# Half of the context's features transposed in 32x32 blocks by VectorE from a second copy, in place of TensorE's transposes

## The reference, cut to what matters

```
x: (16, 64, 512)   ctx: (16, 512, 512)                 # 16 batches, 64 queries, 512 context rows, 512 features
q = layernorm(x) @ Wq.T + bq
k = ctx @ Wk.T + bk ;  v = ctx @ Wv.T + bv
scores = (q @ k.T) / sqrt(512)
keep the 32 largest scores of each query, the rest -inf; attn = softmax(scores)
x = x + (attn @ v) @ Wo.T + bo
```

## Time and profile before

| | |
|---|---|
| median of 3 runs | 445.98 us (445.91 to 446.12) |
| the profiled execution's own time | 447.19 us |
| its span, first to last instruction | 445.4 us |
| granted TensorE clock | 1.00 (2.4 GHz) |
| PE busy | 433.1 us, 97% of the span |
| DVE busy | 257.6 us, 58% |
| ACT busy | 205.6 us, 46% |
| DMA | 49.97 MB, mean 112 GB/s |

### The profile page before, as it was taken

How to read it: one execution, slowest core, us unless ns; L and a number is a source line. 1 busy time by engine, 2 the same in 40 slices (tenths; PEclk the granted TensorE clock), 3 DMA queues, 4 the chain that set the end, 5 groups by cost and what they waited for, 6 DMA issues and landing times.

```text
span 445.4 us, 5681 instructions
## 1 busy us (share of the span) xinstructions
PE 433.1 (97%) x2045; PEld 312.7 (70%) x2045; DVE 257.6 (58%) x519; ACT 205.6 (46%) x305; POOL 111.1 (25%) x163
## 2 busy tenths in 40 slices
PE   5999999999999999899999999999999999999996
PEld 2587644557565655478888888887888888888884
DVE  2988535567766777769987335548753333533334
ACT  1796852645464466538875445435531111111110
POOL 2600440000000002010008603334256633333330
PEclk9999999999999999999999999999999999999999
DMA  6999920675414542225649000000000000200002
GB/s 192 409 379 391 371 80 0 208 266 190 179 46 155 190 156 105 94 96 188 213 166 177 13 22 4 0 0 1 0 1 0 0 1 1 95 1 1 1 0 94
DMA packets 26844, 49.97 MB, mean 112 GB/s; under 512 B 6208, under 2 KB 6208, under 8 KB 25792
## 3 DMA queue, kind: packets, MB, share of 16 engines
q1 hardware_dynamic: 26816, 49.61, 31.7%
HBM read 47.49 MB, written 2.11 MB: 111 GB/s over the span
## 4 chain that ended last, share of the span: by engine, by line
PE 78%; DMA 7%; DVE 6%; ACT 4%; issue 2%; SPq 1%; POOL 1%; DVEq 0%; ACTq 0%
PE bank L1189 10%; PE bank L1191 10%; PE bank L1190 10%; PE bank L1605 7%; PE bank L1603 7%; PE bank L1589 6%; PE bank L1590 6%; PE bank L1384 6%; PE bank L1370 5%; PE bank L1398 5%; PE bank L1297 3%; PE bank L1196 3%; DMA wab<-w1T 2%; DMA wab<-w2T 2%; DVE ln_s L779 1%
## 5 line engine op out<-in xcount | busy, mean ns | idle before, releaser
L754 ACT ACTIVATE g<-bank,b1c 128x512 f32<-128x512 f32 x32 | 22.0, 688 | 92.0 <-PE bank L1605 92.0
L1169 DVE CAST g_hi<-g 128x512 fp32r<-128x512 f32 x32 | 14.0, 436 | 74.7 <-ACT g L754 74.6
L417 POOL TENSOR_TENSOR ln_rs<-ln_ve,neg_half 128x1 f32<-128x1 f32 x24 | 14.9, 620 | 146.2 <-DVE ln_ve L783 145.8
L1603 PE MATMUL bank<-xt_lo,w1s 128*128 128x512 f32 x128 | 50.8, 397 | 0.0
L1605 PE MATMUL bank<-xt_hi,w1s 128*128 128x512 f32 x128 | 50.7, 396 | 0.0
L1589 PE MATMUL bank<-w2s,g_lo 128*128 128x512 f32 x128 | 50.3, 393 | 0.2 <-DVE g_lo L1171 0.2
L1590 PE MATMUL bank<-w2s,g_hi 128*128 128x512 f32 x128 | 50.0, 390 | 0.0
L569 ACT ACTIVATE mt<-bank 128x512 f32<-128x512 f32 x56 | 30.1, 600 | 28.6 <-PE bank L1370 28.6
L464 POOL TENSOR_SCALAR w2s<-w2t 128x512 fp32r<-128x512 int8 x32 | 19.9, 622 | 65.8 <-PE bank L1590 65.8
L1384 PE MATMUL bank<-mt,qT 128*64 128x512 f32 x128 | 31.1, 605 | 0.0
L1589 PEld LDWEIGHTS bank<-w2s,g_lo 128*128 128x128 f32 x128 | 24.0, 188 | 6.1 <-issue 0.6
(11 more groups left out here) (231 smaller groups left out, 1015.3 us busy)
## 6 DMA issues: line engine op xcount, KB each, us to landing
ctxr<-ctx SPq DMA_DIRECT2D x8, 1024.0 KB, 10.9
ctx<-ctx SPq DMA_DIRECT2D x8, 1024.0 KB, 7.7
wab<-w1T SPq DMA_DIRECT2D x4, 1024.0 KB, 11.5
wab<-w2T SPq DMA_DIRECT2D x4, 1024.0 KB, 9.0
wgraw<-wgT SPq DMA_DIRECT2D x4, 1024.0 KB, 6.5
wst<-w1T SPq DMA_DIRECT2D x4, 1024.0 KB, 4.7
wst<-w2T SPq DMA_DIRECT2D x4, 1024.0 KB, 5.2
resid<-x SPq DMA_DIRECT2D x4, 512.0 KB, 6.9
```

What stands on the lines that cost most here:

```text
L1603: pe.matmul(bank[n % 2][:, :], w1s[:, n % 2, d, :], xt_lo[:, d, half(n // FC)], start=(d == 0), stop=False)
```

## The change

The context's features 0 to 255 are loaded a second time, in another layout: `raw_load(i)` loads for pair `i`, in four DMAs of 32 partitions each, rows in blocks of 32, so that partition 32g+j holds row 32m+j of each block m with the features 64g to 64g+63. Such a DMA moves 256 bytes at a time. DVE then transposes 32x32 blocks (`block_part`, two instructions of 128x512 for a quarter of the features, four a pair), which gives the turned context for features 0 to 255 in another order of the features; `m1_hi`, `m1_lo` and `sum_k` are put into the same order (`blocks_first`, `in_blocks`), for which each `m1` part is split into two instructions of 256 columns on ACT and on DVE. PE turns only the features 256 to 511: four chunks a pair, two in each half of an iteration. ACT copies all four; DVE's `mt1_part` is gone. The steps of the score take the pieces in the order 2, 0, 3, 1: first and third from ACT, second and fourth from DVE.

The second copy takes two of the eight tiles, so that three pairs of the context are held and not four; `ctx_load` waits for a `weigh` one iteration later than before relative to its use, and `raw_load` for the transposes that free its tile. DVE's list in an iteration is reordered (in the diff). `wgraw`, `wst`, `qfT`, `conv`, the `toe` tiles and `woutraw` move to other tiles, with waits to match; `woutraw` now waits for the last `ternary`.

```diff
+BLK = 32
...
-        (ctxr,), (wgraw,), (wk_lo,), (qfT, conv), (wst,) = region(
+        (ctxr,), (wgraw,), (wk_lo, wgq_lo), (conv, qfT), (wst,) = region(
             [("ctxr", [P, 4, SC, D], F32)],
             [("wgraw", [P, 4, DC, D], F32)],
-            [("wk_lo", [P, DC, D], F32R)],
-            [("qfT", [P, DC, B * T], F32), ("conv", [P, NT, D], F32)],
+            [("wk_lo", [P, DC, D], F32R), ("wgq_lo", [P, DC, D], F32R)],
+            [("conv", [P, NT, D], F32), ("qfT", [P, DC, B * T], F32)],
             [("wst", [P, 4, FF], F32)])
         (ctx2,), \
             (xn6, targ, tdec, habs, cpr, wpar, wtmp, cpl, tpos), \
-            (wv_hi, wv_lo, wgq_lo), (toe_hi, toe_lo, _, woutraw), (wave_hi, wave_lo) = region(
+            (wgraw2, wv_hi, wv_lo), (wst2,), (_, woutraw, toe_hi, toe_lo), (wave_hi, wave_lo) = region(
             [("ctx2", [P, 4, SC, D], F32)],
             [("xn6", [P, NT - 2, D], F32), ("targ", [P, H, CT], F32), ("tdec", [P, H, CT], F32), ("habs", [P, H, NC], F32),
              ("cpr", [P, P], F32), ("wpar", [P, 3, H], F32), ("wtmp", [P, 6, H], F32), ("cpl", [P, H], F32),
              ("tpos", [P, CT], F32)],
-            [("wv_hi", [P, DC, D], F32R), ("wv_lo", [P, DC, D], F32R), ("wgq_lo", [P, DC, D], F32R)],
-            [("toe_hi", [P, H, P], F32R), ("toe_lo", [P, H, P], F32R), ("apart", [P, DC, D], F32),
-             ("woutraw", [P, DC, D], F32)],
+            [("wgraw2", [P, 2, DC, D], F32), ("wv_hi", [P, DC, D], F32R), ("wv_lo", [P, DC, D], F32R)],
+            [("wst2", [P, 2, FF], F32)],
...
+        def ctx_home(b):
+            return (2, 3, 5, 6, 0, 1)[b % 6]
...
+            n = ctx_home(b)
+            return (ctx2 if n < 4 else ctxr)[:, n % 4, :, :]
+        def raw_pair(i):
+            return ctxr[:, 3 * (i % 2), :, :].rearrange("p c d -> p (c d)").rearrange("p (m e) -> p m e", e=2 * BLK)
+        def blocks_first(row):
+            return row.rearrange("p (g q i) -> p q g i", q=2, i=BLK)
+        def in_blocks(row):
+            return row.rearrange("p (q g i) -> p q g i", q=2, i=BLK)
...
+            def raw_load(i):
+                both = ctx[2 * i:2 * i + 2].rearrange("b (m j) e -> j (b m) e", j=BLK)
+                for g in range(4):
+                    sp.dma_start(raw_pair(i)[BLK * g:BLK * g + BLK, :, :],
+                                 both[:, :, 2 * BLK * g:2 * BLK * g + 2 * BLK]).then_inc(raw_in[i % 2], 16)
+            def ctx_load(b):
+                sp.dma_start(ctx_tile(b), rows(ctx[b])).then_inc(ctx_in[b % 6], 16)
+            raw_load(0)
+            ctx_load(0)
+            ctx_load(1)
+            for k in range(3, 2 * DC):
+                if k == 2 * DC - 2:
+                    sp.dma_start(wvraw[:, :, :], rows(wv)).then_inc(wv_in, 16)
+                abs_load(k)
+            raw_load(1)
+            for b in range(2, 4):
+                ctx_load(b)
+            sp.dma_start(b1c[:, :], small[1]).then_inc(small_in, 16)
+            sp.dma_start(bqg[:, :, :], small[2]).then_inc(small_in, 16)
+            for i in range(2, NT):
+                sp.wait_ge(block_ok, DC * (i - 1))
+                raw_load(i)
+                if i == 2:
                     sp.wait_ge(ctok_ok, 1)
                     sp.wait_ge(mix_ok, 1)
                     sp.wait_ge(norm_ok, 1)
-                if b >= 8:
-                    sp.wait_ge(am_ps, b // 2 - 3)
-                sp.dma_start(ctx_tile(b), rows(ctx[b])).then_inc(ctx_in[b % 8], 16)
-                if b == 1:
-                    for k in range(3, 2 * DC):
-                        if k == 2 * DC - 2:
-                            sp.dma_start(wvraw[:, :, :], rows(wv)).then_inc(wv_in, 16)
-                        abs_load(k)
-                if b == 3:
-                    sp.dma_start(b1c[:, :], small[1]).then_inc(small_in, 16)
-                    sp.dma_start(bqg[:, :, :], small[2]).then_inc(small_in, 16)
-                if b == 4:
+                else:
+                    sp.wait_ge(am_ps, i - 2)
+                ctx_load(2 * i)
+                ctx_load(2 * i + 1)
+                if i == 3:
...
+                if n == 0:
+                    sp.wait_ge(block_ok, DC * (NT - 1))
+                elif n == 1:
+                    sp.wait_ge(am_ps, NT - 2)
+                elif n == 3:
+                    sp.wait_ge(block_ok, DC * NT)
+                sp.dma_start(wg_tile(n), rows(wgT[n])).then_inc(wg_in[n], 16)
...
+            sp.wait_ge(tern_ok, 2 * DC)
             sp.dma_start(woutraw[:, :, :], rows(woutT)).then_inc(wout_in, 16)
...
-                act.activation(m1_hi[:, e, :], bank[e][:, :], ACT.Copy).then_inc(m1_hi_ok, 1)
+                act.activation(in_blocks(m1_hi[:, e, 0:D // 2]), blocks_first(bank[e][:, 0:D // 2]),
+                               ACT.Copy).then_inc(m1_hi_ok, 1)
+                act.activation(m1_hi[:, e, D // 2:D], bank[e][:, D // 2:D], ACT.Copy).then_inc(m1_hi_ok, 1)
...
-                act.wait_ge(ctx_turned, 2 * DC * i + j + 1)
-                if i or j >= 4:
-                    act.wait_ge(scored, DC * i - 1 + j // 2)
-                act.activation(mt[:, j % 4, :], ctx_bank(j)[:, :], ACT.Copy).then_inc(mt_ok, 1)
+                act.wait_ge(ctx_turned, DC * i + j + 1)
+                if i or j >= 2:
+                    act.wait_ge(scored, DC * i + 2 * (j // 2) - 1)
+                act.activation(mt[:, j % 2, :], ctx_bank(DC * i + j)[:, :], ACT.Copy).then_inc(mt_ok, 1)
...
                 mt_part(i, 0)
-                mt_part(i, 2)
-                mt_part(i, 3)
+                mt_part(i, 1)
...
-                mt_part(i, 4)
-                mt_part(i, 5)
-                mt_part(i, 6)
-                mt_part(i, 7)
+                mt_part(i, 2)
+                mt_part(i, 3)
...
-                dve.tensor_tensor(m1_lo[:, e, :], bank[e][:, :], f(m1_hi[:, e, :]),
+                dve.wait_ge(m1_hi_ok, 2 * e + 2)
+                dve.tensor_tensor(in_blocks(m1_lo[:, e, 0:D // 2]), blocks_first(bank[e][:, 0:D // 2]),
+                                  in_blocks(f(m1_hi[:, e, 0:D // 2])), ALU.subtract).then_inc(m1_lo_ok, 1)
...
-            def mt1_part(i):
-                dve.wait_ge(ctx_turned, 2 * DC * i + 2)
-                if i:
-                    dve.wait_ge(scored, DC * i - 1)
-                dve.tensor_copy(mt[:, 1, :], ctx_bank(1)[:, :]).then_inc(mt1_ok, 1)
+            def block_part(i, q):
+                if q == 0:
+                    dve.wait_ge(raw_in[i % 2], 64 * (i // 2 + 1))
+                if i or q:
+                    dve.wait_ge(scored, DC * i + 2 * q)
+                else:
+                    dve.wait_ge(q_ps, 2 * DC)
+                for par in range(2):
+                    dve.transpose(out=mt[:, 2 + par, :].rearrange("p (m i) -> p m i", i=BLK),
+                                  in_=raw_pair(i)[:, 16 * par:16 * par + 16, BLK * q:BLK * q + BLK]).then_inc(block_ok, 1)
 
             for i in range(NT):
-                if i == 1:
-                    wvo_lo_part(2)
-                if i >= 2:
-                    top8(i - 1, 2)
-                mt1_part(i)
-                if i == 1:
-                    top8(i - 1, 2)
+                block_part(i, 0)
                 if i == 0:
                     wvo_lo_part(0)
+                    block_part(0, 1)
+                    continue
+                top8(i - 1, 0)
+                top8(i - 1, 1)
+                if i == 1:
+                    wvo_lo_part(1)
+                    wvo_lo_part(2)
+                top8(i - 1, 2)
+                top8(i - 1, 3)
                 if i >= 2:
                     amt_lo_part(i - 2)
-                if i >= 1:
-                    top8(i - 1, 3)
-                    kept_part(i - 1)
+                kept_part(i - 1)
+                rinv_part(i - 1)
+                block_part(i, 1)
                 if i >= 3:
                     xt_lo_part(NT + i - 3, i - 3, ln2_bank(i - 3))
-                if i >= 1:
-                    rinv_part(i - 1)
                 if i == 1:
                     wvo_lo_part(3)
                     scales()
@@ -1046,11 +1099,9 @@
                     ln2_stats(i - 2)
                 if i == NT - 1:
                     split_lo(0, wk_lo, wk_hi)
-                top8(i, 0)
-                top8(i, 1)
-                if i == 0:
-                    wvo_lo_part(1)
+            top8(7, 0)
+            top8(7, 1)
...
+                n, b, d = DC * i + j, 2 * i + j % 2, 2 + j // 2
+                if j < 2:
+                    pe.wait_ge(ctx_in[b % 6], 16 * (b // 6 + 1))
+                if n >= 3:
+                    pe.wait_ge(mt_ok, n - 2)
                 else:
-                    pe.wait_ge(q_ok, (5, 6, 8)[j])
+                    pe.wait_ge(q_ok, (5, 6, 8)[n])
                 for c in range(SC):
-                    ins = pe.transpose(ctx_bank(j)[:, token(c)], ctx_tile(b)[:, c, token(d)], ident[:, :])
```

(44 more changed lines are left out.)

79 lines of the change are left out of this document (27 added, 52 removed).

## The result

The changed kernel takes 451.0 us, the median of 4 runs (450.8 to 453.13), beside 445.95 for the kernel before in runs alternating with them: a ratio of 1.0125, with a 95% interval of 1.0094 to 1.0156. It is 5.05 us slower. The profiled run took 450.86 us, with a span of 448.9.

The account below looks back on a forecast made before the run. Full DMA queue bounds the start, PE the iterations from 2 on, DVE's chain close behind. +5.5 - 1.0 - 5 x 0.6 + 0.25 = +1.75 us: 447.7 on the median, 448.9 on the profiled run; range 443.5 to 452.

Parts of the forecast that it names:

- copy at the start, until the first score: Start: `raw_load(0)`, 1.05 MB at 192 GB/s, delays the last query and first score by 5.5 us, range 2.7 to 6.5.
- iterations 0 and 1: First two attention iterations: fewer PE transposes, mostly hidden by ACT's copies, save 1.0 us together, between 0 and 2.5.
- iterations 2 to 6 and the first half of 7: Five iterations each 0.6 us shorter, then +0.25 us for the first half of iteration 7.
- end: Attention behind `project(5)`: the chain gets no shorter; PE's 0.9 us saving becomes a longer wait for `prob`, about 2.5 us.
- the rival of cheap small pieces: Start: copy runs near the rate of large pieces, costing 2.7 to 4 us; total 444.9 to 446.2; chance 0.22.
- slow transposes: Rival, chain to `project`: block transposes above 0.68 us cost their excess 12 times; at 1.10 us, 452.8 total; chance 0.17.
- The m1 split: Start: eight `m1` instructions of 256 columns for four of 512 on ACT and DVE cost 0; uncovered, about 1 us.
- The steady iterations: From iteration 2: `project` waits for DVE's `amt_lo`, 8.25 us behind the scores; 14.5 us per iteration, 0.6 less.
- The loads in the iterations: Steady iterations: 11 us of loads, second copy included, fit in 14.5 us; cost 0.
- The rival that PE's saving arrives whole: Steady iterations: if DVE's chain didn't hold `project`, six iterations save 1.8 us each; total 441.5; chance 0.06.

Follow-up runs that it names:

- the gap filled: Changed kernel with `wvo_step(0)` put ahead of the first score in PE's list, and a wait for `abs_ok` ahead of ACT's copy: 446.62 us.
- the late copy: Changed kernel with `raw_load(0)` issued behind `abs_load(6)`, not ahead of the context of batch 0: 450.64 us; with `amt_lo` also one place earlier, 444.95 us.

## Why the prediction was right in direction and short in size

The forecast was +1.75 us, with 446.9 to 449.5 as its own range; the measured 451.0 lies outside that and inside the whole range of 443.5 to 452. The terms, measured on the spans 443.6 and 448.9:

| step | forecast | measured | from |
|---|---|---|---|
| copy at the start, until the first score | +5.5 | +6.3 | 57.84 - 51.53 |
| duration of the first scores | none | +1.8 | 3.68 - 1.87 |
| iterations 0 and 1 | -1.0 | -0.9 | pair 1's scores 87.31 - 80.06 = 7.25, less the two above |
| iterations 2 to 6 and the first half of 7 | -2.75 | -2.0 | 84.72 - 86.68 between pair 1's scores and the last `add_att` |
| end | 0 | 0 | span behind that `add_att`: 276.87 and 276.86 |
| sum | +1.75 | +5.2 | 448.9 - 443.6 = 5.3 |

These are differences of single profiles. Three more kernels have the changed kernel's lists up to the first score, which starts at 58.65, 58.94 and 59.31 there, after 57.84; in the kernel before it started at 51.53 and 53.28. So the first row is good to a microsecond or more. The second is firmer: the score took 3.68, 3.44, 3.68 and 3.62 us in these four.

**The step that failed** is that "the last query and the first score come 5.5 us later", as the whole price of the copy. As a delay it was mis-sized by 0.8, no more than the scatter, and stayed below the upper bound of 6.5: the landing of `abs_load(3)` moved by 42.81 - 36.39 = 6.4 us, so 1.05 MB went at 164 GB/s, and the stretch 27.4:31.7 shows 162, where the prediction had taken the 192 of the `toe` tiles. That was one microsecond of their load, before the DMA was fully busy (share 0.95). The stretches behind it in the same trace have 183 and then twice 171, which makes 5.7 to 6.1 us:

```profile
238.00:239.00 1.00, 1.00 (x6) 0.82 (x5) 1.00 (x2) 1.00 (x2) 0.95 (x1) 1.00 1.28 183
239.00:240.00 1.00, 1.00 (x6) 0.81 (x5) 1.00 (x2) 0.05 (x1) 0.95 (x1) 1.00 1.35 171
240.00:242.00 2.00, 2.00 (x11) 1.59 (x10) 1.93 (x3) 1.27 (x2) 2.00 (x2) 1.00 1.37 171
```

What was missing is the term behind it. The prediction let PE stand still for the delay and put nothing for what PE does afterwards. It comes back at half its clock and loses another 1.8 us; with the gap filled (the run with `wvo_step(0)` moved) the first score has 1.94 us again. The split into bytes (2.8) and pieces (3.6) puts an end to the rival of cheap small pieces. That the measured time still lies inside the whole range is luck: the upper part of that range was there for slow transposes, and they weren't slow. The Trainium skill, "DMA: Bandwidth & Descriptors", section "Why small descriptors are slow (HBM only)", gave an estimate of 3.8 us for the whole copy; this case's traces do not agree, with a delay of 6.4.

**The m1 split** was right at nothing for the changed kernel: eight instructions on DVE take 2.75 us (22.32 to 25.07) for 2.48, and the chain of waits runs through SP's issuing of the copy there. The cover is that issuing itself. In the kernel before, the chain runs through ACT's copies of `m1` (22.06 to 24.01), and in the one with the late copy through the eight that take their place (22.06 to 24.26): there the split costs 0.25 us.

**The steady iterations** were right in kind and nearly in size: 14.63 us for 14.5, by errors that cancel. `project` starts 7.80 us behind the scores' copy and not 8.25: DVE's transposes need not wait for that copy and begin 0.13 ahead of it, so that the first MAX8 starts 1.10 behind it and not 1.35, and the four `top8` steps take 5.97 and not 6.2. From `project` to the next scores it takes 6.83 and not 6.25. The eight transposes of the two chunks do take half of the 1.75 us of the sixteen (127.45 to 128.32), but then PE waits 0.30 for ACT's copies of them, and ACT copies the scores 0.25 after they are complete, since `ln2_apply` stands ahead of that and waits for its layer norm. The experiments hold both signs of it: `amt_lo` moved forward gives 0.91 per iteration, transposes doubled in the first half cost 1.33, in the second 0.29. The 0.7 us that had been estimated from the Trainium skill, "VectorE: DVE Perf Modes", section "The three transpose paths", agrees with the 686 ns of the trace.

**The loads in the iterations** were right at nothing: no wait of DVE for the DMA stands in the iteration, and large pieces left it at 14.63. **The end** was right at nothing: PE waits 2.11 us for `prob`, 2.5 had been forecast, and the 0.5 more than before costs nothing: from the transposes of `prob` on, the span lasts another 264.06 us in both kernels.

**The rival that PE's saving arrives whole** counted 1.8 us in an iteration if DVE's chain didn't hold `project`. With `amt_lo` moved it doesn't, and 15.09 became 13.72, 1.37 less; then the clock at the end of the attention took 1.6 us of it back.

What stays open: why the clock fell behind the wait for the last `prob` in some profiles and not in others (below), and whether a place in the queue exists where the copy costs nothing at all. Not tried was a first pair turned on TensorE as before, which would need no copy at the start.

## What to carry to other kernels

A second load of data that the chip already gets is priced where the queue is full, by what is issued behind it: the transfer's time at the rate of its piece size, measured where the DMA is fully busy, the time that its issue holds the queue, and what the starved engine loses after it restarts. When work is taken off the busiest engine, write out the chain of the engine that receives it, since the order of its list decides how much arrives: here two entries of DVE's list exchanged were worth 4 us, nearly as much as the whole change cost. And take a second profile before pricing a stage by one: the first one here was 1.8 us long in the very stage in question.

## What the runs showed of the hardware that had not been expected

- Waiting costs TensorE twice. Behind a gap of 4.77 us the granted clock was 0.50, 1.2 GHz, and eight multiplications took 3.68 us for 1.87. At the end of the attention the length of the wait for `prob` doesn't tell whether it falls. Behind 2.73 us it fell to 0.66 in one profile and stayed at 1.00 in two others with 2.72 and 2.71; behind 2.11 us it stayed in the changed kernel and fell to 0.69 and 0.71 in two others (the gap filled, the first transposes doubled). Where it fell, the span behind the last `add_att` of the loop is 278.4 to 278.5 us; where it stayed and ACT's list wasn't edited there, 276.9 to 277.0, whatever the wait: the fall costs 1.5 to 1.6 us. In the 12 runs of the late copy with `amt_lo` the time goes with the mean granted clock (only the 442.99 has a profile, so where the others lost it isn't shown): 442.65 and 442.99 at 0.996, 443.21 to 444.39 at 0.992, 445.51 to 446.04 at 0.988, 446.25 and 447.74 at 0.985. The copy in large pieces does so too: 446.8 at 0.996, 449.36 to 450.19 at 0.989. The kernel before, at 1.00 in its profile, spreads over 1.1 us in 24 runs.
- Pieces of 256 bytes from HBM moved 162 GB/s at a DMA share of 1.36 (27.4:31.7), and 171 to 183 at 1.28 to 1.37 in the `toe` load of the kernel before (238 to 242 us), whose large pieces moved 356 to 421 at 0.95 to 1.06 from 13 to 49 us; 1.05 MB of them delayed the load behind by 6.4 us, in pieces of 2 KB by 2.8.
- Issuing four such DMAs held SP's list for 16.5 us while the DMA was full, 8.6 us with pieces of 2 KB, and 2.7 and 4.2 in two iterations in the middle (from 111.92 and 126.56 on). The loads behind them in the list are delayed by the issue and not only by the transfer.
